# Expert results scattered plainly into two arrays and added to rows in SBUF by GpSimd's adding transfers; weight loads on SyncE spread over the tiles

## The reference

```python
x = x + 0.5 * ffn(layernorm(x))
x = x + attn(layernorm(x))
x = x + 0.5 * ffn(layernorm(x))
# ffn: 8 experts, 2 chosen for each token
scores, idx = top_k(softmax(x @ Wg), 2); scores /= scores.sum(-1, keepdims=True) + 1e-8
expert_out[e] = (silu(x @ W11[e]) * (x @ W12[e])) @ W2[e]          # 256 -> 512 -> 256
out = sum(scores[k] * expert_out[idx[k]] for k in (0, 1))
# attn: RMS norm, in_w gives x and gate, a convolution of width 3 and a 256x256 map,
#       a forward and a backward recurrence of 64 states each, gate, out_w, plus its own input
```

## Time and profile before

| | us |
|---|---|
| median of three runs | 1028.68 |
| the profiled execution, its own time | 1028.27 |
| its span, from the first to the last instruction | 1026.4 |
| PE busy | 914.3 |
| DVE busy | 591.1 |
| POOL busy | 607.3 |
| ACT busy | 340.2 |
| adding scatters of round 0 on POOL, 71 | 116.5 |
| the same in round 1, 71 | 115.2 |

### The profile page before, as it was taken

One profiled execution on the slowest core, in us unless ns is written; L12 is line 12 of the kernel. 1 busy time (PEld: TensorE's weight loads), 2 busy tenths in 40 slices (PEclk: granted clock), 3 DMA queues, 4 the chain that ended last, 5 costly groups with the idle time before them and its releaser, 6 DMA issues.

```text
span 1026.4 us, 20394 instructions
## 1 busy us (share of the span) xinstructions
PE 914.3 (89%) x5386; PEld 780.3 (76%) x5390; DVE 591.1 (58%) x1447; ACT 340.2 (33%) x699; POOL 607.3 (59%) x549
## 2 busy tenths in 40 slices
PE   7658899999999899976997994699999999999995
PEld 7647787878878788864774773478888888888884
DVE  3765565556656565546766875855555555555552
ACT  5743342333423333311327531023322332233221
POOL 3415666767667677734305760167777777777673
PEclk9969999999999999998999995699999999999999
DMA  9576547365363654323212548133344333433332
GB/s 315 195 264 187 150 89 195 77 168 160 79 188 73 179 131 95 49 32 103 63 41 86 186 156 347 45 71 77 53 74 77 56 72 53 79 76 52 52 50 30
DMA packets 78275, 116.06 MB, mean 113 GB/s; under 512 B 12048, under 2 KB 61072, under 8 KB 77904
## 3 DMA queue, kind: packets, MB, share of 16 engines
q0 software_dynamic: 31808, 37.83, 23.1%
q1 hardware_dynamic: 32896, 51.92, 14.8%
q10 hardware_dynamic: 13520, 25.70, 7.3%
HBM read 70.99 MB, written 48.63 MB: 117 GB/s over the span
## 4 chain that ended last, share of the span: by engine, by line
PE 60%; DVE 11%; issue 8%; POOL 6%; ACT 5%; DMA 4%; ACTq 3%; SPq 2%; POOLq 0%; another core or an unknown queue 0%; DVEq 0%
PE bank L1412 32%; PE bank L1435 16%; PE bank L1421 5%; PE bank L1404 3%; POOL seq L466 2%; PE bank L1533 2%; DVE work L834 2%; DMA xg<-xn_rows,idx_i 1%; SPq L306 1%; DVE sg L1078 1%; ACTq L648 1%; DVE bnst L822 1%; ACTq L646 1%; DVE w_lo L1143 1%; ACT sg L657 1%
## 5 line engine op out<-in xcount | busy, mean ns | idle before, releaser
L1078 DVE TENSOR_TENSOR sg<-sg,bank 128x512 f32<-128x512 f32 x142 | 97.7, 688 | 309.0 <-ACT sg L657 256.9
L1412 PE MATMUL bank<-w_hi,xt_hi 128*128 x568 | 241.3, 425 | 25.3 <-DVE xt_lo L1067 19.0
L1412 PE MATMUL bank<-w_hi,xt_lo 128*128 x568 | 224.6, 395 | 0.0
L1412 PE MATMUL bank<-w_lo,xt_hi 128*128 x568 | 222.8, 392 | 0.0
L649 ACT ACTIVATE yb<-bank,gates_in 128x256 f32<-128x256 f32 x142 | 67.4, 475 | 454.1 <-issue 234.0
L477 POOL DMA_INDIRECT xg<-xn_rows,idx_i x142 | 142.6, 1004 | 98.4 <-DVE idx_i L921 55.8
L481 POOL DMA_INDIRECT gates_in<-gate_rows,idx_g x142 | 138.6, 976 | 55.3 <-issue 42.3
L1435 PE MATMUL bank<-w_hi,ft_hi 128*128 x568 | 160.0, 282 | 7.7 <-ACT yb L649 7.7
L490 POOL DMA_INDIRECT x_rows<-yb,idx_i x71 | 116.5, 1641 | 82.5 <-ACT yb L649 30.5
L1435 PE MATMUL bank<-w_hi,ft_lo 128*128 x568 | 160.5, 283 | 0.0
L1435 PE MATMUL bank<-w_lo,ft_hi 128*128 x568 | 159.0, 280 | 0.0
(11 more groups left out here) (250 smaller groups left out, 1251.5 us busy)
## 6 DMA issues: line engine op xcount, KB each, us to landing
xn_rows<-work SPq DMA_DIRECT2D x16, 512.0 KB, 3.0
w_lo_rows<-w_lo ACTq DMA_DIRECT2D x16, 512.0 KB
w_lo<-w_lo_rows SPq DMA_DIRECT2D x16, 512.0 KB
work<-x_rows SPq DMA_DIRECT2D x16, 512.0 KB, 3.8
w_lo<-w_lo_rows SPq DMA_DIRECT2D x2, 4096.0 KB, 17.5
x_all<-x SPq DMA_DIRECT2D x8, 512.0 KB, 9.3
w_lo_rows<-in_sb ACTq DMA_DIRECT2D x16, 256.0 KB
out_rows<-seq SPq DMA_DIRECT2D x8, 512.0 KB, 3.3
```

What stands on the lines that cost most here:

```text
L1078: nc.vector.tensor_tensor(sg[p], sg[p], ps_g[p][:], ALU.mult).then_inc(f_step, 1)
L1412: last = nc.tensor.matmul(dst[p][:], xt[p][:, c, :], of(w), start=(c == 0 and n == 0), stop=(c == DC - 1 and n == len(parts) - 1))
```

## The change

In round 0 the results are no longer added in DRAM. A token's first choice goes to row n of a new array `y_rows`, its second to row 4096 + n, and no row is written twice: the scatters are plain and wait only for `yb`. For each chunk of the mixer's forward half SP loads the rows of x, POOL adds the two rows of results to them in SBUF with two adding transfers (`add_y`), one after the other, and SP stores the sum to `x1_rows`. POOL's queue holds these transfers of chunk i + 2 behind the factors of chunk i. The norm of the forward half moves from DVE to ACT; the backward half's two passes of ACT become one, and its two additions of POOL one.

The loads of weights and the stores of the up weights' low parts move from ACT's queue to SP's, each at a named tile, the high and low parts are made in pieces of 512 columns, one or two at a tile, and the down weights land in `w2_hi` itself, from where ACT copies them to a staging buffer before it rounds them. POOL gathers two tiles further ahead at a round's start. Before round 0 the norm of chunks 0 to 3 goes to DVE, with three buffers in place of two, and the copy of the input to `x1_rows` goes.

```diff
+        def load_slot(q, j):
+            if j > 0:
+                for landed in (w11_in, w12_in, w2_in):
+                    q.wait_ge(landed, 16 * j)
+            e = expert_of_slot(q, j)
+            load_up(q, j, e)
+            load_down(q, j, e)
...
-            sp.dma_start(x1_dram[0:L, :].rearrange("(p t) d -> p (t d)", p=P), x.rearrange("(p t) d -> p (t d)", p=P)).then_inc(x1_out, 16)
...
+            def load_ahead(j, tile):
+
+                sp.wait_ge(ye_done, tile + 1)
+                load_slot(sp, j)
+
+            load_ahead(1, 1)
+            store_up_lo(0)
+            load_ahead(2, 5)
+            load_w2_lo(0, 1)
+            load_ahead(3, 9)
...
+            for p in range(2):
+                sp.wait_ge(y_out[p], 16 * ((ET + 1 - p) // 2))
+            sp.wait_ge(lo_out, 32 * E)
+            load_x1(0, 0)
+            load_x1(1, 1)
+            for i in range(NCH):
+                b = i % 2
+                sp.wait_ge(summed, 16 * (i + 1))
+                sp.dma_start(rows(x1_dram, i), xin[b]).then_inc(x1_out[b], 16)
+                if i + 2 < NCH:
+                    sp.wait_ge(norm_ready, i + 1)
+                    sp.wait_ge(x1_out[b], 16 * (i // 2 + 1))
+                    load_x1(i + 2, b)
...
-                nc.gpsimd.tensor_tensor(x2[b], xin[b], t_rows[b], ALU.add).then_inc(res_step, 1)
-                pool.wait_ge(res_step, i + 1)
-                nc.gpsimd.tensor_tensor(x2[b], x2[b], outb_sb[:].unsqueeze(1).to_broadcast([P, G, D]), ALU.add).then_inc(res_ready, 1)
+                nc.gpsimd.tensor_tensor(x2[b], t_rows[b], outb_sb[:].unsqueeze(1).to_broadcast([P, G, D]), ALU.add).then_inc(res_ready, 1)
...
+                    if r == 0:
+                        nc.gpsimd.indirect_dma_start(y_dram, bass.IndirectOffsetOnAxis(ap=idx_s[:, t:t + 1], axis=0), yb[t % 2], None).then_inc(y_out[t % 2], 16)
+                        return
...
+            def add_y(i, b, k):
+
+                if k == 0:
+                    pool.wait_ge(x_in[b], 16 * (i // 2 + 1))
+                else:
+                    pool.wait_ge(half_sum, 16 * (i + 1))
+                nc.gpsimd.dma_start(xin[b], y_dram[k * L + i * CH:k * L + (i + 1) * CH, :].rearrange("(j p) d -> p j d", p=P),
+                                    accum_op=ALU.add).then_inc(half_sum if k == 0 else summed, 16)
...
+            for i in range(NCH):
+                rsqrt_rms(i, i % 2)
+                if i + 2 < NCH:
+                    add_y(i + 2, i % 2, 0)
+                    add_y(i + 2, i % 2, 1)
...
+            def high_down(j, h):
+
+                at_ = w2_hi[:, j * IC + 2 * h:j * IC + 2 * h + 2, :].rearrange("p c d -> p (c d)")
+                act.wait_ge(w2_in, 16 * (j + 1))
+                if j > 0:
+                    act.wait_ge(w2_lo_out, 16 * j)
+                nc.scalar.activation(w2_stage[h], at_.bitcast(F32), ACT.Copy).then_inc(staged, 1)
+                act.wait_ge(staged, 2 * j + h + 1)
+                nc.scalar.activation(at_, w2_stage[h], ACT.Copy).then_inc(hi2_ready, 1)
...
-                    if s == 0:
-                        load_up(act, j, expert_of_slot(act, j))
...
+                    if s in (1, 2):
+                        high_down(j, s - 1)
                     if s == 4:
-                        high_value(j)
-                    if s == 5:
-                        high_down(j)
-                    if s == 7:
                         store_low(j)
+                    if s in (3, 4):
+                        high_up(j, s - 3)
+                    if s in (5, 6):
+                        high_value(j, s - 5)
```

More of the change, by code:

```diff
@@ L202, in build @@
         pad, token = part(6576, ET), part(6647, ET)
+        row_of, in_p, in_t = (part(at, ET).bitcast(I32) for at in (1779, 1850, 1921))
+        pad_rows = part(7097, ET)
         past_end, past_ends = part16(6718, ET + 1, E - 1)[:, 0:ET], part(6718 + 252, ET)
@@ L312, in _ @@
             sp.wait_ge(const_ready, 1)
-            for dram in (xn_dram, x1_dram, out):
+            for dram in (xn_dram, out):
                 sp.dma_start(dram[L:ROWS, :], zeros).then_inc(pads_out, 16)
@@ new lines, in _ @@
+            load_ahead(1, 1)
[3 more added lines that the diff above has]
+            load_ahead(3, 9)
+            store_up_lo(1)
+            load_ahead(4, 13)
+            load_w2_lo(0, 2)
+            store_up_lo(2)
+            load_ahead(5, 16)
+            load_ahead(6, 19)
+            load_ahead(7, 22)
+            for j in range(3, E):
+                load_w2_lo(0, j)
+                store_up_lo(j)
+            sp.wait_ge(w2_lo_in, E * 16)
@@ L392, in _ @@
             store_gates(1)
-            load_w2_lo(1)
-            sp.wait_ge(pads_out, 48)
+            for j in range(E):
+                load_w2_lo(1, j)
+            sp.wait_ge(w2_lo_in, E * 16 * 2)
+            sp.wait_ge(pads_out, 32)
             for b in range(2):
                 sp.wait_ge(x_out[b], 16 * (NCH // 2))
-                sp.wait_ge(xn_out[b], 16 * NCH)
-            sp.wait_ge(added, 2 * 16 * ET)
+                sp.wait_ge(xn_out[b], 16 * (NCH // 2))
+            sp.wait_ge(added, 16 * ET)
         @block.gpsimd
@@ L721, in gate_out, with norm_x1 @@
                                          bias=col[:, C_INB + DC + jc:C_INB + DC + jc + 1]).then_inc(xz_ready, 1)
+            def norm_x1(i, b):
+                act.wait_ge(rstd_ready, i + (NCH + 1))
+                if not (isinstance(i, int) and i < 2):
+                    act.wait_ge(tr_done, i - 1)
+                for t in range(G):
+                    last = nc.scalar.activation(xn[b][:, t, :], xin[b][:, t, :], ACT.Identity, scale=rstd[:, b, 1, t:t + 1], bias=rstd[:, b, 0, t:t + 1])
+                last.then_inc(norm_ready, 1)
             for i in range(2):
-                rows_high(i, i)
+                norm_x1(i, i)
+            rows_high(0, 0)
+            rows_high(1, 1)
+            norm_x1(2, 0)
             gate_out(0)
-            with act.Fori(0, NCH // 2 - 1) as j:
+            norm_x1(3, 1)
+            with act.Fori(0, NCH // 2 - 2) as j:
                 for b in range(2):
@@ L729, in _ @@
                     gate_out(j * 2 + (b + 1))
+                    norm_x1(j * 2 + (b + 4), b)
+            for i in range(NCH - 2, NCH):
+                rows_high(i, i % 2)
+                gate_out(i - 1)
             gate_out(NCH - 1)
@@ L828, in ln_stats, with apply_x @@
                 last.then_inc(mv_ready, 1)
+            def apply_x(k):
+                dve.wait_ge(rstd_ready, k + 1)
+                if k >= 3:
+                    dve.wait_ge(xn_x_out[k % 3], 16 * (k // 3))
+                for t in range(k * G, (k + 1) * G):
+                    last = nc.vector.tensor_scalar(xn_x[k % 3][:, t % G, :], x_all[:, t, :], x1_rstd[:, t:t + 1], x1_mean[:, t:t + 1], ALU.mult, ALU.add)
+                last.then_inc(norm_dve, 1)
             def ln_apply(k, b, src, which=0):
@@ L1087, in experts @@
                 if r == 0:
-                    low_up(0)
-                    low_value(0)
-                    dve.wait_ge(pads_out, 48)
+                    for c in range(DC):
+                        low_up(0, c)
+                    for c in range(DC):
+                        low_value(0, c)
+                    dve.wait_ge(pads_out, 32)
                     rows_in(0, 0)
@@ L1095, in experts @@
                     nc.vector.tensor_copy(v(UB), ps_w[:, D:D + 1]).then_inc(wct_ready, 1)
-                    low_down(0)
+                    for h in range(2):
+                        low_down(0, h)
                     gates(0)
@@ L1199, in _ @@
                 stats_x1(b, 0, b)
-            for b in range(2):
-                norm_x1(b, b)
             dve.wait_ge(m_ready, 1)
@@ L1205, in _ @@
             stats_x1(2, 1, 0)
-            norm_x1(2, 0)
             rows_low(1, 1)
```

313 lines of the change are left out of this document (159 added, 154 removed).

## The result

The kernel after takes 1136.74 us (median of 4 runs, 1130.91 to 1140.25) and the kernel before 1029.18 beside it (4 runs, 1026.73 to 1032.29). The ratio is 1.104, 95% interval 1.098 to 1.109: slower by a tenth. The forecast was 1082, range 1040 to 1110. The direction was right and the size was not; the time lies above the range.

A forecast was written before the change was run, and what follows sets the result against it. PE had little slack in either mixer half, and weights' work cost round 0 23.8 us. From 1028.3: -5.5 + 11 - 18 - 1.6 + 73.6 + 2 - 8 = 1081.8, stated as 1082, range 1040 to 1110.

The forecast's parts named there:

- A: Before round 0: norms shared with DVE and a third buffer start the gathers earlier, -5.5 us.
- B: Wait at tile 2: slot 1's down weights land late, ACT's piece holds up sg and PE idles before tile 3, +11 us.
- C: Rest of round 0: even loading wins back most of the weights' cost, 25.9 less 8 for pieces, -18 us.
- The even loading doesn't do what it says: Rival, round 0: pieces ahead of sg and the wait at tile 2 eat the 18 us gain, 1100; chance 0.08.
- D: Last scatter of round 0: plain and without waiting for the one before, it lands sooner, -1.6 us.
- E: Mixer's forward half: adding transfers make chunks run one after another, period 16.6 us, +73.6 us and +2 for the clock.
- F: Mixer's backward half: less POOL work per chunk and a shorter start of the chain, -8 us.
- G: Routing and round 1: three more small DVE operations against two gathers that come earlier, 0 us.
- not slower: Rival, forward half: transfers come near their latency, period 10.5 us, whole kernel 1026; chance 0.08.
- cheap adding transfers: Rival, forward half: adding transfers cost their fixed time alone, 3.6 us and 1.0 on POOL, whole 1050; chance 0.22.
- issue grows with rows: Rival, forward half: POOL pays for each row, 6.6 us a transfer, period 25.2, whole 1147; chance 0.10.
- The case with 0.52: The forecast itself, forward half: adding transfers of 5 to 8 us, whole from 1062 to 1102; chance 0.52.

The follow-up runs named there:

- e2_down1: Kernel after with the load of slot 1's down weights alone issued ahead of round 0: 1113.75 us, ratio 1.085 to the kernel before.
- after_again: Kernel after, unchanged, run again in another set: 1114.68 us, ratio 1.089 to the kernel before.
- b3_spread: Kernel after without the two arrays, value pieces earlier, slot 1's down weights loaded early, SyncE's loads one at a time and later: 1019.58 us, ratio 0.990.
- e8_delay: Kernel after with earlier value pieces, slot 1's down weights early, loads one at a time, four small GpSimd additions ahead of each plain scatter: 1078.55 us.
- e3_order: Kernel after with GpSimd's forward-half order changed: first adding transfer of chunk i+1, factors of chunk i, second transfer of i+1: 1110.94 us, ratio 1.082.
- e4_plain: Kernel after with GpSimd's transfers of results in the mixer made plain, leaving out the adding: 1106.82 us, ratio 1.078.
- after_third: Kernel after, unchanged, run again in another set: 1136.11 us, ratio 1.104 to the kernel before.
- after_fourth: Kernel after, unchanged, run again in another set: 1137.15 us, ratio 1.106 to the kernel before.

## Why the prediction was right or wrong

*A and B, to tile 3: right.* Forecast +5.5 for its start on PE, measured 95.01 - 88.41 = +6.6. The first transposes of `xg` come at 65.48 in place of 71.29, 5.8 earlier (forecast 5.5). From there B took 12.4, forecast 11, and e2_down1 gives 10.3 to 12.6 for the same wait. ACT stood 15.7 us and PE 13.0, not the 7 named as the sign: the delay was forecast, the idle time around it was not.

*C, the rest of round 0: wrong, and this is the step that failed.* "25.9 - 8 = 18" was gained on paper. Of it 2.1 lay between tile 3's start and its result, which took 0.5 us more instead, and the rest in tiles 3 to 70, which came out 28.5 longer, 44.5 from the forecast. The step counted what pieces cost as work ahead of `sg`, "three tiles of eight lose 0.3 to 0.5", and took a slot's last tile for one like the others. It isn't: the low value piece stands on DVE behind `fu` of that tile, `fu` needs its last product, and PE waits for the piece ahead of the next slot's first product. PE therefore stops in each of seven slots for 2.2 to 3.8 us, 21.6 in all, and its clock falls with it. With the piece and nearly without the rhythm the stretch takes 356.9 us (after_again), 22 to 23 more than the 335.0 and 334.3 of b3_spread and e8_delay, where both are absent: that is the piece's price, 3.8 in the slots between and less in the first and the last. The other 21.5, 378.5 - 356.9, came with the rhythm, which no row of before shows; its cause stays open. The forecast's 334 holds where both are absent, but in kernels that differ in other edits, too (loads one at a time, no wait at tile 2), so its closeness is in part luck. Even with hardly any rhythm the kernel took 1114.68 (after_again), above the range of 1040 to 1110. "The even loading doesn't do what it says" was a rival, but with a price of 18, as nothing gained; it had no term for a loss. The place could be read from the order in advance: which tile has the last piece, and what waits for it.

*D: right.* -1.6 forecast, -2.0 measured.

*E, the forward half: right.* +73.6 and +2 forecast, +77.1 measured. An adding transfer landed in 6.0 (forecast 6.4), POOL's issue took 1.28 to 1.42 (1.6), the period was 15.9 to 18.7 (16.6), and e3_order shows that POOL's order made it serial. The norm of chunk 7 came at 629.75 + 2.08, 136.5 after the load was issued (forecast 133.1), and 22.0 us followed it (21.9). So the clock of 0.73 in this half cost nothing behind the last norm; the added 2 us were right by chance: they covered part of the 3.4 that the chain ahead of that norm took longer than forecast. The landing was taken from rows, 0.126 us for an added row, and came near. From the Trainium skill (DMA: Bandwidth & Descriptors, Anatomy of one DMA), about 2.0 us and the bytes over 436 GB/s, an estimate of 3.2 us for 512 KB follows. The traces disagree: e4_plain shows 4.2 for the plain transfer and the kernel after 6.0 for the adding one. The measurement decides.

*F, the backward half: right in kind, too large.* -8 forecast, -2.7 measured. The cycle fell from 8.5 to 8.0 us a chunk, not to 7.8. At the start 3 to 4 us were to be gained and 2 were lost: POOL's first factors of this half come 671.40 - 653.86 = 17.5 us after PE's last product, before 558.42 - 543.17 = 15.3. The first four products of `woc` took 3.48 us and before 1.98, with PE's clock low behind the forward half (timeline of PE):

```profile
656.51 3.48 PE L1682 MATMUL bank<-states,woc_sb 128*128 128x512 f32 x4 [2.67 <-DVE states L1334]
```

The stretch around them, with a granted clock of 0.86:

```profile
656.00:668.00 12.00, 8.91 (x24) 4.89 (x24) 5.73 (x8) 7.61 (x15) 4.69 (x2) 0.86 0.16 54
```

This varies: after_third and after_fourth took 1.98 and 1.99 us for the group, and from PE's last forward product to the last one of `woc` 58.2 and 57.7 us, where the profiled execution took 59.5 and before 60.8. So a part of F's shortfall belongs to this one execution.

*G and the end.* Routing with the start of round 1 +1.6, round 1 -1.0, forecast 0. Behind the last result 3.5 more, which had no term.

Of the chances, "not slower" and "cheap adding transfers" fell by the landing of 6.0, "issue grows with rows" by POOL's 1.28 to 1.42. The case with 0.52, transfers of 5 to 8 us, is the one that came true, and its range from 1062 to 1102 failed by round 0 alone. The whole range ended at 1110 since no case let round 0 lose.

## What to carry to other kernels

When work is spread over the tiles of a loop, look first at the piece that ends last before a wait and count that wait, the 1.2 us of the sequencer behind it and the clock, for the mean cost of a piece says nothing of it. Where short transfers wait for one another, spread the large loads beside them: it made the difference between 352 and 335 us here. Two executions of one kernel can differ by 21.5 us in a single stretch, so compare within a set and stretch by stretch.

## What the hardware showed that was not expected

- A rhythm of two tiles, 6.7 and 4.25 us for 4.87 each, in which ACT starts 1.45 us and more after the transposes that it waits for. Its cause is open.
- A GpSimd transfer of 512 KB into SBUF lands in 4.2 us when plain and 6.0 when adding (medians of 16). Of two adding ones issued 0.8 us apart the first landed after 5.9 and the second after 7.8; beside a load and the next adding one it was up to 9.1.
- From the start of the last result to the end of the execution's own time, thirteen executions with the two arrays take 11.2 to 12.5 us, before and the kernels without them 7.6 to 9.1. No row shows what it is.
